# Order of a SyncE queue and steps of one projection in an attention and mixture-of-experts kernel

## The reference

```python
h = einsum('bsd,bsde->bse', base_embeddings[x], rule_transform[token_rules[x]])
a = layernorm(h)
q = einsum('btd,hrd->bhtr', a, Q); k = einsum('bud,hrd->bhur', a, K)      # H=8, R=32
attn = softmax(einsum('bhtr,bhur->bhtu', q, k) / sqrt(64))
h = h + einsum('bhtd,hde->bte', einsum('bhtu,bud->bhtd', attn, a), VO)
h = h + ffn(layernorm(h))          # gate, top 2 of 8 experts, relu(x W1 + b1) W2 + b2, weighted sum
```

## Time and profile before

| | |
|---|---|
| median of 3 runs | 612.52 us (608.01 to 615.87) |
| the profiled execution, whole | 610.8 us |
| its span in the profile | 608.8 us |
| TensorE matmul busy | 81% of the span |
| VectorE busy | 68% |
| ScalarE busy | 47% |
| GpSimd busy | 38% |

### The profile page before, as it was taken

One profiled execution on the slowest core, in us unless ns is written; L12 is line 12 of the kernel. 1 busy time (PEld: TensorE's weight loads), 2 busy tenths in 40 slices (PEclk: granted clock), 3 DMA queues, 4 the chain that ended last, 5 costly groups with the idle time before them and its releaser, 6 DMA issues.

```text
span 608.8 us, 9495 instructions
## 1 busy us (share of the span) xinstructions
PE 495.7 (81%) x2764; PEld 270.0 (44%) x2764; DVE 411.8 (68%) x1003; ACT 287.2 (47%) x581; POOL 229.1 (38%) x375
## 2 busy tenths in 40 slices
PE   0168404878777888999999999999999999999985
PEld 0036302444442334445544544554454445576663
DVE  5634288883126756888868968986984876755477
ACT  0205101037663535465565565555566545547673
POOL 5765356462425200431352254032322313181542
PEclk9999665579998997999999999999999999999988
DMA  8825210919620171532330431134042200000000
GB/s 237 316 65 168 62 35 28 210 57 232 195 79 18 35 171 36 123 74 63 82 76 2 104 90 34 30 90 101 2 104 63 52 2 11 1 10 2 11 2 17
DMA packets 21792, 47.05 MB, mean 77 GB/s; under 512 B 6249, under 2 KB 11577, under 8 KB 21681
## 3 DMA queue, kind: packets, MB, share of 16 engines
q1 hardware_dynamic: 15408, 32.23, 21.9%
q0 software_dynamic: 4752, 8.20, 4.5%
q10 hardware_dynamic: 1584, 6.03, 3.0%
HBM read 9.97 MB, written 11.01 MB: 34 GB/s over the span
## 4 chain that ended last, share of the span: by engine, by line
PE 55%; DVE 18%; POOL 9%; issue 8%; DMA 4%; ACT 4%; SPq 2%; DVEq 0%; ACTq 0%; POOLq 0%
PE bank L1304 15%; PE bank L1290 10%; PE bank L1266 7%; POOL ctxT L522 5%; PE bank L1214 4%; PE bank L1236 4%; DVE mx L1009 4%; DMA ctxT<-in_table,ids 2%; PE bank L1208 2%; PE bank L1209 2%; DVE r_sb L1067 2%; POOL r_sb L595 2%; POOL emb_sorted L532 1%; PE bank L1315 1%; PE bank L1249 1%
## 5 line engine op out<-in xcount | busy, mean ns | idle before, releaser
L1009 DVE TENSOR_REDUCE mx<-bank 128x1 f32<-128x512 f32 x256 | 170.7, 687 | 79.0 <-PE bank L1290 72.8
L595 POOL TENSOR_TENSOR r_sb<-r_sb 128x256 f32<-128x256 f32 x174 | 90.9, 523 | 248.9 <-DVE r_sb L1085 168.5
L675 ACT ACTIVATE prob<-bank 128x512 f32<-128x512 f32 x256 | 138.8, 597 | 68.7 <-PE bank L1266 56.3
L1304 PE MATMUL bank<-prob,xa 128*64 128x512 f32 x448 | 123.5, 630 | 0.0
L1290 PE MATMUL bank<-ks,qs 96*128 96x512 f32 x240 | 111.4, 467 | 13.9 <-DVE mx L1009 13.8
L1290 PEld LDWEIGHTS bank<-ks,qs 96*128 96x128 f32 x240 | 46.2, 193 | 121.8 <-issue 103.4
L1266 PE MATMUL bank<-qs,ks 97*128 97x512 f32 x224 | 77.3, 427 | 0.0
L742 ACT ACTIVATE r_sb<-bank,stay 128x512 f32<-128x512 f32 x56 | 37.1, 687 | 44.9 <-PE bank L1209 44.6
L1266 PEld LDWEIGHTS bank<-qs,ks 97*128 97x128 f32 x224 | 38.6, 194 | 15.3 <-issue 10.5
L522 POOL DMA_INDIRECT ctxT<-in_table,ids x32 | 33.2, 1036 | 22.5 <-DMA ctxT<-in_table,ids 9.6
L532 POOL DMA_INDIRECT emb_sorted<-ctxT,pos x32 | 32.3, 1009 | 20.4 <-DMA emb_sorted<-ctxT,pos 12.2
(11 more groups left out here) (173 smaller groups left out, 696.2 us busy)
## 6 DMA issues: line engine op xcount, KB each, us to landing
qs<-qk_h SPq DMA_DIRECT2D x64, 128.0 KB, 2.5
ks<-qk_h SPq DMA_DIRECT2D x56, 128.0 KB, 2.5
qs<-qk_l SPq DMA_DIRECT2D x32, 128.0 KB, 2.5
ks<-qk_l SPq DMA_DIRECT2D x28, 128.0 KB, 2.4
emb_sorted<-front ACTq DMA_DIRECT2D x4, 608.0 KB, 9.7
y_sorted<-y_out POOLq DMA_DIRECT2D x19, 128.0 KB, 2.4
e_in<-emb_sorted POOLq DMA_DIRECT2D x9, 256.0 KB, 4.0
emb_sorted<-front ACTq DMA_DIRECT2D x3, 640.0 KB, 9.7
```

The source lines that it names most:

```text
L595: nc.gpsimd.tensor_tensor(a[:, at:at + width], src[:, 0:width], src[:, width:2 * width], ALU.add).then_inc(S["pool_chain"], 1)
L675: nc.scalar.activation(prob[:, step % NPROB, u % 2, :], bank[u % NST][:], ACT.Exp, scale=SC).then_inc(S["exp_done"], 1)
L1009: V.tensor_reduce(mx[:, u // 16, at_:at_ + 1], score_bank(n)[:], AX.X, ALU.max).then_inc(S["mx_done"], 1)
L1304: last = M(bank[5][64 * hh:64 * hh + 64, :], xa[:, b % XAR, ut, :], prob[:, step, hh, :], start=(ut == 0), stop=(ut == J - 1))
```

## The change

Three places change, all in stage 1 (`b == 1`) or for the batches that it serves.

1. In the table, `xT` of batch 3 goes from step 4 to step 8 of stage 1, its four `proj` pieces from steps 5 to 8 to steps 9 to 12, and `rt` of batch 0 from step 6 to step 8. Nothing else in stage 1 is moved.
2. On SyncE, `max_row(1, 1)` is sent as the first thing of iteration 1, ahead of the sums' row of batch 0. Before, it was sent behind `stack(2, 3)`.
3. On SyncE, `stack(2, 2)` is issued in iteration 1, behind the sums' row, and no longer at the end of iteration 0.

```diff
         def x_at(nb):
-            return {1: (-1, 15), 2: (0, 14)}.get(nb, (nb - 2, XT))
+            return {1: (-1, 15), 2: (0, 14), 3: (1, 8)}.get(nb, (nb - 2, XT))
         def proj_at(nb):
-            return {1: ((0, 0), (0, 0), (0, 1), (0, 1)), 2: ((0, 15), (0, 15), (0, 15), (0, 15))}.get(
+            return {1: ((0, 0), (0, 0), (0, 1), (0, 1)), 2: ((0, 15), (0, 15), (0, 15), (0, 15)),
+                    3: ((1, 9), (1, 10), (1, 11), (1, 12))}.get(
                 nb, [(nb - 2, k) for k in PROJ])
...
-            if k == RT and 0 <= b - 1 < B:
+            if k == (RT if b != 1 else 8) and 0 <= b - 1 < B:
                 todo.append(("rt", b - 1, 0))
...
             for b in range(-2, B):
+                if b == 1:
+                    max_row(1, 1)
                 if 0 <= b - 1 < LAST:
...
                     sp.wait_ge(S["srow_in"], 32 * b)
+                if b == 1:
+                    stack(2, 2)
                 if 0 <= b + 1 < B:
                     stack(b + 1, 3)
-                if 0 <= b < B:
+                if 0 <= b < B and b != 1:
                     max_row(b, 1)
...
-                if 0 <= b + 2 < B:
+                if 0 <= b + 2 < B and b != 0:
                     stack(b + 2, 2)
```

## The result

The changed kernel takes 617.33 us (median of 20 runs, 614.09 to 621.62), the kernel before 612.88 us (20 runs, 608.01 to 619.16). The ratio is 1.0078, interval 1.005 to 1.0107: 3.1 to 6.6 us slower. Forecast were 614.5 us and +2.9 us, with 608.5 to 618.5 as the range.

The account below looks back on a forecast made before the run. TensorE, busy 81% of the span, bounds the kernel through its restarts after waits. 610.8 us plus 0.3 (restart) and 2.6 (clock) make 613.7, or 615.4 on the median; 614.5 was taken, range 608.5 to 618.5.

Parts of the forecast that it names:

- the likeliest case: TensorE restarts 0.3 us later in step 15, and the clock falls only behind that wait, 2.6 us; chance 0.45.
- rival 3: The clock falls in both stalls of stage 1, projections take 12 us or more: 617 to 618 us; chance 0.12.
- Part 1, the early row of maxima: Stage 1, SyncE: batch 1's row ready at 222.46, landing at 224.26; batch 3's first cast can start at 236.33.
- Part 2, the stall moved and shortened: ScalarE's first cast of batch 3 waits 4.3 us instead of 7.1; TensorE idles about 2.5 us in step 10.
- The clock behind the first wait: After TensorE's idle time of 2.5 us in step 10, no fall of the granted clock was taken.
- The 10.8: Microseconds from batch 3's first cast to the end of its fourth subtraction, set by VectorE; bounds 9.4 and 12.
- The stacks of batch 3: SyncE issues stack(3, 0) and stack(3, 1) before batch 2's first row of maxima: 2 x 3.80 = 7.6 us.
- The landing of the row behind them: Batch 2's first row of maxima, issued at 254.7, lands 1.80 us later at 256.5.
- The restart in step 15: TensorE idles 4.8 us before L1266, then restarts at 256.5, 0.3 us later than before.
- The clock behind the second wait: After the idle time before step 15, about 6.8 us at half clock near 256 us, costing 2.6 us.
- The estimate from the Trainium skill: Slow stretch before step 15 priced at length times one minus clock ratio: 3.4 us, making the sum +3.7.
- Rival 2: The lead survives: batch 2's row of maxima is not late, TensorE keeps 4.5 to 8 us, about 606; chance 0.13.

Follow-up runs that it names:

- the two edits: The changed kernel with batch 2's first row of maxima ahead of batch 3's first two stacks, and stack(2, 2) at its old place: together 605.6 us, ratio 0.9894.

## Why the prediction was right, and where it was off

The direction came as forecast, and 617.33 us lies in the range. But it was not the likeliest case (0.45, with 614.5 us) that happened. It was rival 3, in which the clock falls in both stalls: it had a chance of 0.12 and gave 617 to 618. Held against the steps of the prediction:

- **Part 1, the early row of maxima: right.** With the 1.34 us taken off, the row left at 222.46 (forecast 222.46 for its data), the sums' row followed 1.83 us later (1.80), the first stack 2.62 behind that (2.62), the second 3.76 (3.80). The cast started at 237.82 - 1.34 = 236.48 (236.33).
- **Part 2, the stall moved and shortened: right.** The profile's wait of 5.29 us begins where ScalarE had nothing left to do; from the end of the first projection (233.77) it is 4.05, forecast 4.3. TensorE idled 2.36 us for it (2.5).
- **The clock behind the first wait: wrong.** I took no fall, since no row had an idle time as short as 2.5 us. It fell, at 239.1. This stretched the four projections from 10.8 to 12.67 us. The 10.8 itself was right, and so was its reason: at full clock it is 10.71 in two runs, and VectorE's part is 10.09 us in the second of them (forecast 10.1). But the 10.76 of before that stood beside it had a slow stretch in it; without one it is 8.53. So the crowding did add 2.2 us, and the prediction's comparison hid them.
- **The stacks of batch 3: 7.6 us was too little.** It was 8.46 (250.52 to 258.98), since one issue took 1.49 us instead of 0.59.
- **The landing of the row behind them: 1.80 was too little.** It was 2.63 (258.98 to 261.61).
- **The restart in step 15.** The sum said 0.3 us later than before. It was 261.64 - 1.34 - 256.24 = 4.06 later. The missing parts are 1.9 (projections), 0.9 (issue), 0.8 (landing) and 0.2 (first issue of the second stack to cast, 5.81 instead of 5.65), together 3.8.
- **The clock behind the second wait: right, its price a little high**, 2.6 against 2.1 us. The estimate from the Trainium skill (TensorE: Matmul & The Clock Gate, section on HAM oscillation) was 3.4. The traces of two kernels say 2.0 to 2.2, as part of the slow stretch lies in idle time.
- **Two sums don't come out.** Rival 3's terms add up to 616.4 to 617.4, not 617 to 618, and the likeliest case's own range from its bounds would be 612.0 to 617.1, not 611.9 to 617.5. Neither changes the forecast.

4.06 and 2.11 make the +6.17 of the profiled stretch; forecast were +2.9. So the queue's part of the mechanism, both waits and their order, was as predicted; the clock behind the first wait was not, and two more terms (the stacks, the landing) were too small. Behind the stretch little changes: the two executions are 7.5 us apart at step 7 of stage 2 and 8.0 at the end. The timed difference, 3.1 to 6.6 us, lies in between, with the forecast just below its lower end and the profiled stretch just inside its upper one.

Executions of the changed kernel spread over 7.5 us. The clock is part of this. At the end of stage 0 TensorE idles 1.8 us in every kernel, for the projections of batch 2. Behind that the granted clock fell in seven of the thirteen traces, that of the changed kernel among them, and stayed up in six, that of the kernel before among them. From there to the copy of step 3 it takes 11.38 us in the changed kernel (207.31 to 218.69) and 10.37 before (206.98 to 217.35), so about 1.0 of the 1.34 us is this fall and not the change. Over the 20 executions the longer ones also tend to have the lower mean granted clock (0.910 in the longest, of 621.6 us, 0.928 in the shortest, of 614.1). That this makes the whole spread was not shown, since only one execution of each kernel has a trace.

Rival 2 (the lead survives) was not what happened, but it named what a lead needs: a row of maxima that is not late. That was so when the row was moved ahead of the stacks and `stack(2, 2)` went back: 605.6 us. That the rival had said about 606 is luck, since its own condition did not hold (the fourth subtraction by about 242; it ended at 243.70).

What stays open: why the second DMA of `stack(3, 0)` took 1.49 us to issue in the changed kernel (and 1.16 to 1.67 in five of the experiments), and 0.59 in the kernel before. Single issues of other DMAs were as long in two more runs (1.61 and 1.72 us).

## What to carry to other kernels

Where one engine issues all DMAs in order, a transfer's time is that of everything ahead of it, waits included. Before a transfer is moved in such a queue, list behind which wait each later transfer now stands, and when its own reader wants it. Moving the producer of a stack later also moves whatever is queued behind that stack, even when its own data is long ready; here a row that was ready waited 7.2 us.

A wait of which both ends hang on the same event (here the fourth projection) can't be shortened by winning time before it. It must be broken by order. The gains of the two edits then add up: by the stretch they gave 4.5 and 7.6 us alone and 12.6 together. By the ratios it is 2.6, 5.9 and 11.3, and the excess over the sum is within the noise.

## What the runs showed of the hardware

- The granted clock of TensorE fell to 1.2 GHz behind an idle time of only 2.4 us, in the changed kernel and in the runs with the row moved ahead and with the second wait filled. Filling about 2 of these 2.4 us with matmuls kept it at 2.4 GHz. I had expected a fall only from about 4 us of idle time. Behind an idle time of 1.8 us, at the same place in all kernels, it fell in seven of thirteen traces.
- A small row sent into an empty queue had landed for its waiter 1.80 us after its issue (before). Right behind the DMAs of two stacks it took 2.1 to 2.7 us in seven runs (2.63 in the changed kernel, 2.67 with `stack(2, 2)` back, 2.09 in the run with 9 and 3 extra matmuls).
- A slow stretch of about 6.8 us behind a wait cost 2.0 to 2.2 us, and two filled waits turned a kernel that was 0.8% slower into one that is even with before, which keeps its own slow stretch.
